# Last cross attention of a fused decoder layer: scores and turned weights share two PSUM banks, and the order of the tiles changes

## The reference, cut to what matters

```
x = layernorm(x + self_attention(x))
# cross attention, 16 heads
scores = einsum('bhsr,bhlr->bhsl', q_r, k_r)
attn   = softmax(scores, axis=-1)
ctx_c  = einsum('bhsl,bld->bhsd', attn, kv_r)
ctx    = einsum('bhsd,hkd->bhsk', ctx_c, w_kc_kv)      # then @ Wo.T
x = layernorm(x + ctx @ Wo.T)
x = layernorm(x + experts(x))
```

## Time and profile before

| | us |
|---|---|
| median of 3 runs | 896.78 |
| lowest, highest | 894.77, 896.8 |
| the profiled execution | 896.49 |
| its span, first to last instruction | 894.7 |
| PE busy in the span | 844.7 (94%) |
| DVE busy | 629.8 (70%) |
| ACT busy | 280.5 (31%) |
| POOL busy | 143.6 (16%) |

### The profile page before, as it was taken

One profiled execution on the slowest core, in us unless ns is written; L12 is line 12 of the kernel. 1 busy time (PEld: TensorE's weight loads), 2 busy tenths in 40 slices (PEclk: granted clock), 3 DMA queues, 4 the chain that ended last, 5 costly groups with the idle time before them and its releaser, 6 DMA issues.

```text
span 894.7 us, 14657 instructions
## 1 busy us (share of the span) xinstructions
PE 844.7 (94%) x5696; PEld 665.6 (74%) x5696; DVE 629.8 (70%) x1378; ACT 280.5 (31%) x502; POOL 143.6 (16%) x122
## 2 busy tenths in 40 slices
PE   5999999999999989999789989999999999999994
PEld 4977678776776767777568778788888888888873
DVE  3565787878878788788687776756575656566657
ACT  4531143212431124220353522332322333232232
POOL 2014400334013330133340400300000000000021
PEclk9999999999999999999999999999999999999997
DMA  9310000000001000000230004110212020000001
GB/s 337 118 36 2 1 2 1 21 29 17 1 1 48 2 16 1 0 25 4 83 105 0 25 25 154 42 59 1 89 48 65 0 88 27 31 1 1 1 24 71
DMA packets 12686, 35.84 MB, mean 40 GB/s; under 512 B 1488, under 2 KB 2384, under 8 KB 12112
## 3 DMA queue, kind: packets, MB, share of 16 engines
q1 hardware_dynamic: 12624, 34.98, 11.3%
HBM read 30.33 MB, written 2.36 MB: 37 GB/s over the span
## 4 chain that ended last, share of the span: by engine, by line
PE 81%; DVE 12%; issue 4%; ACT 2%; DMA 0%; POOL 0%; ACTq 0%; DVEq 0%
PE ps L243 20%; PE ps L244 19%; PE ps L245 19%; PE ps L1406 6%; PE ps L1486 5%; PE ps L1477 2%; PE ps L1288 2%; PE ps L1462 1%; PE ps L1324 1%; PE ps L1242 1%; DVE small L1090 1%; DVE x2T_all L500 1%; DVE su L508 1%; PE ps L1353 1%; PE ps L1281 1%
## 5 line engine op out<-in xcount | busy, mean ns | idle before, releaser
L508 DVE TENSOR_TENSOR su<-sg,ps 128x512 f32<-128x512 f32 x96 | 66.0, 687 | 131.6 <-PE ps L245 130.3
L243 PE MATMUL ps<-y_hi,f_hi 128*128 128x512 f32 x384 | 151.0, 393 | 0.0
L245 PE MATMUL ps<-y_hi,f_lo 128*128 128x512 f32 x384 | 149.5, 389 | 0.0
L244 PE MATMUL ps<-y_lo,f_hi 128*128 128x512 f32 x384 | 149.4, 389 | 0.0
L372 ACT ACTIVATE sg<-ps 128x512 f32<-128x512 f32 x96 | 57.3, 598 | 258.1 <-PE ps L245 258.1
L736 POOL TENSOR_TENSOR roped<-prod 128x512 f32<-128x512 f32 x64 | 80.9, 1286 | 174.5 <-DVE prod L1035 174.5
L1035 DVE TENSOR_TENSOR prod<-ps,ropeq 128x512 f32<-128x512 f32 x128 | 79.3, 681 | 27.7 <-PE ps L245 27.1
L244 PEld LDWEIGHTS ps<-y_lo,f_hi 128*128 128x128 f32 x384 | 72.1, 188 | 15.2 <-issue 0.5
L243 PEld LDWEIGHTS ps<-y_hi,f_hi 128*128 128x128 f32 x384 | 72.1, 188 | 15.2 <-issue 0.5
L245 PEld LDWEIGHTS ps<-y_hi,f_lo 128*128 128x128 f32 x384 | 72.1, 188 | 15.1
L243 PE MATMUL ps<-xT_hi,a_hi 128*128 128x512 f32 x192 | 78.6, 410 | 2.1 <-DVE xT_lo L960 2.1
(11 more groups left out here) (157 smaller groups left out, 1321.7 us busy)
## 6 DMA issues: line engine op xcount, KB each, us to landing
cb<-routing SPq DMA_DIRECT2D x32, 256.0 KB
f_raw<-in_L_ffn_gate_up_proj SPq DMA_DIRECT2D x8, 768.0 KB, 6.2
f_raw<-in_L_ffn_down_proj SPq DMA_DIRECT2D x8, 384.0 KB, 6.9
xb<-in_x SPq DMA_DIRECT2D x4, 512.0 KB, 4.1
lq<-in_L_xattn_Wq SPq DMA_DIRECT2D x1, 2048.0 KB, 15.2
x2T_all<-in_L_xattn_Wo SPq DMA_DIRECT2D x1, 2048.0 KB, 9.0
x2T_all<-x2T SPq DMA_DIRECT2D x4, 512.0 KB, 3.2
out<-res SPq DMA_DIRECT2D x4, 512.0 KB, 2.6
```

The lines of the kernel that those rows point to most:

```text
L243: pe.matmul(dst, l_hi, r_hi, start=first, stop=False, skip_group_check=check)
L244: pe.matmul(dst, l_hi, r_lo, start=False, stop=False, skip_group_check=check)
L245: return pe.matmul(dst, l_lo, r_hi, start=False, stop=last, skip_group_check=check)
L508: dve.tensor_tensor(su[:, k % 2], sg[:, k % 2], bank(2 * (k % 2) + 1), ALU.mult).then_inc(s_su, 1)
```

## The change

In the last block a tile's scores and its turned weights share one pair of banks: 0 and 1 for even t, 2 and 3 for odd t. With that:

- PE no longer waits in `scores(1)` for the shift of tile 0. `scores(2)` and `scores(3)` wait for `turned(0)` and `turned(1)` on ACT (`s_at`) in place of a shift on DVE.
- On PE `scores(2)` moves ahead of `context(0)`, and `scores(3)` ahead of `project(0)` and `context(1)`.
- On DVE `shift(1)` moves ahead of `normalise(0)`, and `shift(3)` ahead of `residual2(0)` and `normalise(2)`.
- On ACT `expo(1)` moves ahead of `turned(0)`, `context(0)` ahead of the second part of `f_hi_out`, `turned(1)` ahead of its third part and of `expo(2)`, and `expo(3)` ahead of `y_hi_out(1)` and `turned(2)`.

Blocks 0 to 2 keep their banks and their order. No instruction is added or taken away.

```
+    score_bank = lambda b, t: 2 * (t % 2) if b == BLOCKS - 1 else 0
+    turn_bank = lambda b, t: 2 * (t % 2) if b == BLOCKS - 1 else 2
 # ACT, turned(t)
-                act.activation(at[:, t % 2], ps[:, 2:4, :].rearrange("p k (r s) -> p (k r) s", s=P), ACT.Copy)\
+                f = turn_bank(b, t)
+                act.activation(at[:, t % 2], ps[:, f:f + 2, :].rearrange("p k (r s) -> p (k r) s", s=P), ACT.Copy)\
 # ACT, the last block
                 expo(0)
+                expo(1)
                 turned(0)
                 act.wait_ge(s_fload[0], 32)
                 f_hi_out(act, 0, 0)
-                expo(1)
+                context(0)
                 f_hi_out(act, 0, 1)
-                context(0)
+                turned(1)
                 f_hi_out(act, 0, 2)
                 expo(2)
-                turned(1)
+                context(1)
+                expo(3)
                 y_hi_out(act, 1)
-                context(1)
                 turned(2)
-                expo(3)
                 context(2)
 # DVE, shift(b, t)
-                sc = heads(bank(i))
+                sc = heads(bank(score_bank(b, t) + i))
 # DVE, the last block
                 shift(b, 0)
+                shift(b, 1)
                 normalise(b, 0)
-                shift(b, 1)
                 normalise(b, 1)
                 shift(b, 2)
+                shift(b, 3)
                 residual2(b, 0, 6)
                 normalise(b, 2)
-                shift(b, 3)
                 residual2(b, 1, 6)
 # PE, scores(t)
-                if t >= 1:
+                if t >= 1 and following:
                     pe.wait_ge(s_sub, 8 * b + 2 * t)
+                if t >= 2 and not following:
+                    pe.wait_ge(s_at, 4 * b + t - 1)
...
-                            mm = pe.matmul(ps[64 * odd:64 * odd + 64, r, o:o + 64], lq[i, p, c:c + 64],
+                            mm = pe.matmul(ps[64 * odd:64 * odd + 64, score_bank(b, t) + r, o:o + 64], lq[i, p, c:c + 64],
 # PE, turn(t)
-                    mm = pe.transpose(ps[:, 2 + p // 4, (p % 4) * P:(p % 4 + 1) * P], e[:, t % 2, p * P:(p + 1) * P],
-                                      ident[:])
+                    mm = pe.transpose(ps[:, turn_bank(b, t) + p // 4, (p % 4) * P:(p % 4 + 1) * P],
+                                      e[:, t % 2, p * P:(p + 1) * P], ident[:])
 # PE, the last block
                 scores(0)
                 scores(1)
                 turn(0)
+                scores(2)
                 context(0)
-                scores(2)
                 turn(1)
+                scores(3)
                 project(0)
                 context(1)
-                scores(3)
                 turn(2)
```

## The result

The changed kernel took 902.35 us (median of 4 runs, 901.73 to 903.73) against 896.63 before: ratio 1.0075, 95% interval 1.0062 to 1.0088. It is slower by 5.7 us, where the sum had the mark 3.2 us later (899.7 us) and the range went up to 901.8. The profiled execution took 902.95 us, its span 901.2.

What follows compares the result with a forecast made beforehand. TensorE was taken as the bound behind turn(2)'s second half, so the time moves with that instruction. Following waits, queues and low clock put it 3.2 us later: 896.49 + 3.2 = 899.7 us, range 897.2 to 901.8.

Steps and rivals of the forecast that it cites:

- the sum: Steps from shift(0) to turn(2) in the last cross attention, added up: 3.2 us later, 899.7 us, chance 0.40.
- the mark: Start of the second half of turn(2) in the last cross attention: 460.59 before, 463.80 forecast.
- The bound: Behind the second half of turn(2), TensorE was said to set the time, busy 20.00 of 20 us from 462 to 482.
- the direction: Whole kernel: slower was given 0.50, same 0.47, faster 0.03.
- The high clock rival: First pair of tiles: TensorE's clock stays high or is back by 448; +1.7 us, 898.2, chance 0.22.
- the free products: VectorE's normalise products of tiles 0 to 2 no longer stretched beside POOL: 2.1 us gained, 1.0 of it in normalise(2).
- The wait of residual2(0): On VectorE, residual2(0) was to wait for project(0) longer than the 1.56 us of before.
- the exponentials of tile 3: Beside scores(3) and project(0), they were to end by 458 and cost nothing.
- the low clock: TensorE in the first pair: half clock through scores(2) and 1.0 us of context(0), called the unknown term.
- low clock until `turn(1)`: Rival: context(0) takes up to 3.96 us, all at low clock; +4.7 us, 901.2; this or further, chance 0.24.
- the last of my signs of being wrong: Behind the second half of turn(2): the forecast is wrong if the lists there do not move by the same amount.
- both kernels have the same list: Behind the second half of turn(2): the kernel's time moves by as much as that instruction, 3.2 us.

Runs made afterwards that it cites:

- e7_after: The changed kernel run again as it is, beside the other experiments' runs of the kernel before: 902.05 us, ratio 1.0079.
- e2_banks: The kernel before with only the shared score and turn banks and their waits changed, all lists in the old order: 896.40 us, ratio 1.0007.
- e9_new_order: The kernel before with normalise(2) ahead of residual2(0) on VectorE and exponentials moved earlier on ScalarE, banks and TensorE's list kept: 892.74 us, ratio 0.9972.
- e5_dense: The changed kernel with extra 128x256 products, results thrown away, in every TensorE hole of the first pair: 898.59 us, ratio 1.0037.
- e3_first: The changed kernel's banks, with its new order for tiles 0 and 1 only and the old order for tiles 2 and 3: 900.37 us, ratio 1.0055.
- e8_queue: The changed kernel with turned(1) ahead of the second part of the expert weights on ScalarE: 901.49 us, ratio 1.0069.
- e11_before_fill: The kernel before with extra thrown-away products between scores(0) and scores(1) and in the hole near 525: 894.85 us, ratio 1.0001.
- e1_fill: The changed kernel with six extra 128x512 products, results thrown away, between scores(1) and turn(0): 901.25 us, ratio 1.0065.

## Why the prediction was wrong

**What held.** The bound (TensorE, full for the first 20 us behind the mark in both kernels), the direction, and the path to the mark: turned(0), scores(2), context(0), turned(1), scores(3), project(0), residual2(0), normalise(2), step by step as in the sum. scores(1) came directly behind scores(0), the hole was 6.16 us where 6 was said, all products of L1097 up to the mark took 0.69. The high clock rival gave 24.1 us from shift(0) to the mark at 462.3; with the clock held it was 24.35. Of the 2.1 us that the free products were to give, only the 1.0 of normalise(2) lies on this path and in the sum. Two readings on the way were wrong and cost the mark nothing. The wait of residual2(0) was to be longer than 1.56 us and was 0.87, because VectorE's wait lay ahead of shift(3), 4.43 us for scores(3). And the exponentials of tile 3 ended at 465.2 and not by 458, behind the copies of context(1).

**The term that was mis-sized: the low clock.** The step was "I take the low clock to last through `scores(2)` and the first microsecond of `context(0)`". It lasted through all of context(0): 3.66 us where the sum had 2.5, and the four transposes and scores(2) were 0.2 and 0.15 longer than the rows of before gave. Start of turned(1): 454.3 expected on this execution's scale, 455.84 measured; mark 463.7 expected, 465.45 measured. I had the bound, the rival "low clock until `turn(1)`" (+4.7; measured +4.95), and gave that and worse 0.24. The rows for the other choice were there and I read them too lightly. The product that still took 0.63 us at 17.14 was the last of twelve that had run since 12.31 without a hole between them.

```profile
12.31 0.77 PE L243 MATMUL ps<-xT_hi,w_hi 128*128 128x512 f32 x1 [1.50 <-DVE xT_lo L960]
```

There some 5 us of solid work had not brought the clock back; in the changed kernel the 5.6 us from the start of scores(2) to the end of context(0) did not either.

**The step that failed: "behind the second half of `turn(2)` both kernels have the same list and TensorE is the bound, so the time moves by as much as that one instruction moves".** The list is the same, but not how long it takes: 1.64 us more, by one fall of the clock behind a hole that both kernels have. None of my cases held that, though the last of my signs of being wrong names it (the lists behind the mark do not move by the same amount); with it the rival's 901.2 becomes 902.8, and the profiled execution was 902.95.
The Trainium skill ("TensorE: Matmul & The Clock Gate", section "HAM oscillation — how this bites in real kernels") says that bursts of matmuls behind waits of some microseconds each start at the low clock. The traces agree for the first pair, by 3.1 us.

**Sum of the loss:** 3.1 clock in the first pair + 2.0 order + 1.6 second fall = 6.7 us; profiled spans 901.2 - 894.7 = 6.5. The median's 5.7 compares 4 runs with 4: of before one was on the lower level, of the changed kernel two (901.73 and 901.74). With more runs beside each other it was 6.6 (e7_after).

**Open.** The fall behind the late hole came in all seven traces of kernels whose mark was 1.9 us or more behind before's and that had no late filler, and in none of before, e2_banks or e9_new_order; the hole is 2.4 us in all. A low stretch earlier in the execution does not decide it: e2_banks had one of 10 us in the first pair and no fall, e5_dense had none there and fell. Nor does the place in the span alone: in e3_first the hole ended at 528.17 and the clock fell, in e2_banks it ended at 528.04 and the clock stayed. Counted from shift(0) the hole ended after 89.5 us or less in the three without a fall and after 91.2 or more in the seven with one. By what rule, the runs do not show. What the 2.0 us of the order consist of is argued from the queue (project(0) behind scores(3), and e8_queue's 0.4), not split further.

## What to carry to other kernels

A hole in TensorE's work can be paid twice, once as idle time if anything waits for it, and again through the clock of what comes behind it. Price a new hole by running everything up to the next solid stretch, and some of that too, at the lower clock, and then look whether anything waits for it: a low clock over the whole first pair cost 3.1 us in one order (e7_after against e5_dense) and at most 0.5 in another (e2_banks, 22.64, against e11_before_fill, 22.11). Before instructions of one engine are moved ahead, ask what is then queued behind their wait: here moving scores(3) ahead, for which nobody waited, put project(0) behind turned(1). The gain lay elsewhere (e9_new_order): some 2 us in having the exponentials ready for normalise(1) and its products at 0.69 us, and at most 1.1 in not letting normalise(2) queue behind a residual that waits for TensorE.

## What had not been expected of the hardware

- Six products with holes of 0.8 to 1.2 us behind them did not keep the clock up (e1_fill); products in those holes did (e5_dense), at no cost in time.
- An identical hole of 2.4 us led to a fall of the clock or not (tails of 434.1 to 434.2 against 435.7 to 435.8 us), though neither its length nor TensorE's list from the mark on differed.
- A VectorE product of two SBUF inputs took 0.69 us while POOL was busy with L334 (e9_new_order, 447.95), where in the kernel before it took 1.09 and 1.50.
- The same program has two levels of time 1.6 us apart; in the traces they go with a clock that is low or not for some microseconds near 55 us. With 4 or 5 runs a median can fall on either, so differences of 0.2% want the profile beside them.
